# Cross-attention decoder on one core: Q and K projected densely and packed by selection matmuls, layer-norm endings on GpSimd, new step orders

## The reference

```
x1 = LN(x  + mha(x,  x,   causal, masks))           # "self",  S
x2 = LN(x1 + mha(x1, ctx, masks))                   # "cross", C
x3 = LN(x2 + fc2(relu(fc1(x2))))                    # tail of C
y  = LN(x3 + Wo(mha(x3, ctx, biased q/k/v)) + bo)   # "outer", O, and its tail
```

## Time and profile before

| what | value |
|---|---|
| median of 3 runs | 459.49 us |
| profiled execution | 457.92 us |
| its span | 456.2 us |
| PE, DVE, ACT, POOL busy | 384.5, 354.0, 249.2, 111.1 us |
| granted PE clock, mean | 0.986 |

### The profile page before, as it was taken

The page is one execution under the profiler, slowest core; times in us unless marked ns, Lnnn a source line. Parts: engine busy times, 40 slices in busy tenths (PEclk is TensorE's granted clock), DMA queues, the critical chain, the costliest instruction groups (busy, mean ns, idle before and its releaser), DMA issues.

```text
span 456.2 us, 10986 instructions
## 1 busy us (share of the span) xinstructions
PE 384.5 (84%) x3512; PEld 280.3 (61%) x3528; DVE 354.0 (78%) x1144; ACT 249.2 (55%) x557; POOL 111.1 (24%) x261
## 2 busy tenths in 40 slices
PE   0477899887898998989989899898998999889863
PEld 0454655665666666757757677676666667667632
DVE  7456888886898887887977888888787788777753
ACT  3024455544665655655665575665665765656632
POOL 8900012111221120321312132221322122322122
PEclk9989999999999999999999999999999999999987
DMA  5022323203322122222222222222122132232310
GB/s 161 0 53 57 81 62 97 60 19 64 86 59 55 39 61 53 46 62 51 45 64 51 47 53 60 46 56 62 42 58 58 40 77 49 52 65 45 67 26 17
DMA packets 22270, 25.62 MB, mean 56 GB/s; under 512 B 3781, under 2 KB 12742, under 8 KB 22214
## 3 DMA queue, kind: packets, MB, share of 16 engines
q1 hardware_dynamic: 22214, 24.93, 24.2%
HBM read 3.61 MB, written 1.05 MB: 10 GB/s over the span
## 4 chain that ended last, share of the span: by engine, by line
PE 43%; DVE 24%; issue 12%; DMA 8%; ACT 7%; SPq 4%; DVEq 0%; POOL 0%; POOLq 0%; ACTq 0%
DVE negmax L653 10%; PE k_bank L367 7%; DMA spread<-negmax_T 7%; PE score L400 6%; PE attend L425 6%; PE o_bank L442 5%; PE o_bank L452 4%; PE q_bank L367 4%; ACT o_sb L539 3%; PE score L403 2%; ACT high_q L585 2%; DVE x L739 2%; ACT high_k L577 2%; SPq L1064 2%; DVE scaled L734 2%
## 5 line engine op out<-in xcount | busy, mean ns | idle before, releaser
L531 ACT ACTIVATE probs<-attend 128x512 f32<-128x512 f32 x192 | 112.0, 599 | 46.5 <-PE attend L425 23.8
L653 DVE TENSOR_REDUCE negmax<-score 128x4 f32<-128x512 f32 x192 | 126.8, 683 | 13.1 <-PE score L403 7.2
L425 PE MATMUL attend<-spread,packed 128*128 128x512 f32 x192 | 91.1, 479 | 18.5 <-DMA spread<-negmax_T 17.3
L400 PE MATMUL score<-spread,packed 128*128 128x512 f32 x192 | 85.9, 484 | 8.0 <-DVE negmax L653 4.5
L577 ACT ACTIVATE high_k<-k_bank,flags 128x512 fp32r<-128x512 f32 x48 | 33.0, 687 | 76.5 <-PE k_bank L367 76.5
L425 PEld LDWEIGHTS attend<-spread,packed 128*128 128x128 f32 x192 | 36.5, 191 | 33.5 <-DMA spread<-negmax_T 23.2
L400 PEld LDWEIGHTS score<-spread,packed 128*128 128x128 f32 x192 | 36.1, 192 | 30.6 <-DVE negmax L653 25.5
L367 PE MATMUL k_bank<-xc_T,w_packed 128*128 128x128 f32 x384 | 52.4, 281 | 1.8 <-ACT xc_T L558 0.5
L367 PE MATMUL q_bank<-xc_T,w_packed 128*128 128x128 f32 x384 | 52.3, 281 | 0.0
L442 PE MATMUL o_bank<-probs,v_aug 128*32 128x128 f32 x1536 | 52.1, 276 | 0.0
L367 PEld LDWEIGHTS k_bank<-xc_T,w_packed 128*128 128x128 f32 x384 | 49.1, 196 | 2.1 <-ACT xc_T L558 0.8
(11 more groups left out here) (120 smaller groups left out, 629.1 us busy)
## 6 DMA issues: line engine op xcount, KB each, us to landing
spread<-packed SPq DMA_DIRECT2D x192, 96.0 KB
out_dram<-y_out SPq DMA_DIRECT2D x16, 64.0 KB, 1.8
spread<-negmax_T SPq DMA_DIRECT2D x48, 16.0 KB
rows_sb<-rows_dram SPq DMA_DIRECT2D x1, 704.0 KB
w_sb<-weights_dram SPq DMA_DIRECT2D x1, 576.0 KB, 4.2
spread<-len_mask SPq DMA_DIRECT2D x32, 8.0 KB
packed<-len_mask SPq DMA_DIRECT2D x32, 8.0 KB
x_in<-x_dram SPq DMA_DIRECT2D x1, 512.0 KB, 3.6
```

The lines of the kernel that those rows point to most:

```text
L400: last = nc.tensor.matmul(dst[:, :], packed[:, s, 0, q, :], spread[:, s, 1, :, q, :], start=True, stop=l != SELF)
L425: last = nc.tensor.matmul(dst[:, :], packed[:, s, 1, q, :], spread[:, s, 0, :, q, :], start=True, stop=l != SELF)
L531: nc.scalar.activation(probs[:, q, :], attend_bank[q % 2][:, :], ACT.Exp, scale=float(DK) ** -0.5).then_inc(exp_done.sem, 1)
L653: nc.vector.tensor_reduce(negmax[:, :].rearrange("p (j q) -> p j q", q=QUADS)[:, :, q], score_bank[q % 2][:, :].rearrange("p (j t) -> p j ...
```

## The change

Q and K come from one dense f32 matmul each (128x128, `qk_ps`). ACT rounds them to high parts and DVE takes the low parts, both on 128x256 instead of twice 128x512. Twelve fp32r matmuls of 256 columns with 0/1 weights (`select_w`, 128x128) place the parts in packed form in two banks; ACT evacuates each (128x512), adding the ones rows as bias. The bias of O goes into ACT's and DVE's instructions as a per-partition column. The endings of the layer norms (two instructions for each) move from DVE to POOL. `v_aug` has 6 slots. The tail's PSUM moves from the Q bank into a third of the transposes' bank. The first scores take the unpacked parts, 3 matmuls for 4. All `step` orders are new, and `w_packed`, `flags` and the bias pieces go.

```diff
# PE
-    project(u + 2, 1) ... project(u + 2, 0)      # 4 + 4 matmuls, 128 columns, f32
+            def project_qk(f):
+                pe.wait_ge(xc_T_ready.sem, xc_T_ready(f))
+                pe.wait_ge(packed_ready.sem, packed_ready(f - 1))
+                for kind, ws in ((0, WQ), (1, WK)):
+                    last = nc.tensor.matmul(qk_ps[:, kind, :], w_sb[:, ws[l], :],
+                                            xc_T[:, 1 if kind and l != SELF else 0, :], start=True, stop=True)
+            def select(f, half):
+                pe.wait_ge(low_ready.sem, low_ready(f))
+                if half == 0:
+                    pe.wait_ge(v_ready.sem, v_ready(f))
+                elif layer_of(f) != OUTER:
+                    pe.wait_ge(len_chain.sem, len_chain(f, 1))
+                for q in range(2):
+                    dst = pack_bank[half][:, 2 * S * q:2 * S * q + 2 * S]
+                    for term, pair in enumerate((parts[:, Q_HIGH:K_HIGH + 1, :], parts[:, Q_HIGH:K_LOW + 1:2, :],
+                                                 parts[:, Q_LOW:K_HIGH + 1:2, :])):
+                        last = nc.tensor.matmul(dst, select_w[:, term, 2 * half + q, :, :], pair,
+                                                start=term == 0, stop=term == TERMS - 1)
# ACT
-    high_k_parts, high_q_parts: 128x512 each
+            def high_parts(f):   # waits for qk_done(f), selected(f - 1), first_done(f - 1)
+                if layer_of(f) == OUTER: # Q and K apart, 128x128 each, ACT.Identity with bias
+                else:
+                    nc.scalar.copy(parts[:, Q_HIGH:K_HIGH + 1, :], qk_ps).then_inc(high_ready.sem, 1)
+            def pack(f, half):
+                act.wait_ge(selected.sem, selected(f, half + 1))
+                act.wait_ge(attended.sem, attended(f - SLOTS))
+                nc.scalar.activation(
+                    packed[:, slot_of(f), :, 2 * half:2 * half + 2, :].rearrange("p a q s -> p q a s"),
+                    pack_bank[half][:, :].rearrange("p (q a s) -> p q a s", q=2, a=2), ACT.Identity,
+                    bias=ones[:, 0:1]).then_inc(packed_ready.sem, 1)
# DVE
-    split_k, split_q: 128x512 each; finish
+            def low_parts(f):    # waits for high_ready(f); O: two scalar_tensor_tensor of 128x128 with the bias
+                    nc.vector.tensor_tensor(parts[:, Q_LOW:K_LOW + 1:K_LOW - Q_LOW, :], qk_ps,
+                                            parts[:, Q_HIGH:K_HIGH + 1, :].bitcast(F32), ALU.subtract)
# POOL, in attention_rstd (the same in tail_rstd, to x3 or y_out)
+                nc.gpsimd.tensor_scalar(normed[:, :], scaled[:, :], rstd[:, 0:1], None, ALU.mult)
+                nc.gpsimd.tensor_tensor(x1[:, m, :], normed[:, :], rows_sb[:, LN1B, :], ALU.add)
```

More of the change, by code:

```diff
@@ L351, in project @@
                 pe.wait_ge(xc_T_ready.sem, xc_T_ready(f))
[L352 to L369, removed]
+                pe.wait_ge(packed_ready.sem, packed_ready(f - 1))
+                if l != SELF:
+                    pe.wait_ge(weights_in_2, 16)
+                for kind, ws in ((0, WQ), (1, WK)):
+                    last = nc.tensor.matmul(qk_ps[:, kind, :], w_sb[:, ws[l], :],
+                                            xc_T[:, 1 if kind and l != SELF else 0, :], start=True, stop=True)
+                last.then_inc(qk_done.sem, 1)
             def project_v(f):
@@ L382, in first_scores @@
                 pe.wait_ge(first_ready.sem, first_ready(f))
-                pe.wait_ge(packed_k.sem, packed_k(f))
-                for q in range(QUADS):
-                    last = nc.tensor.matmul(first_ps, first_q[:, H * q:H * q + H],
-                                            packed[:, slot_of(f), 1, q, :],
-                                            start=q == 0, stop=q == QUADS - 1)
+                for n, (q, k) in enumerate(((Q_HIGH, K_HIGH), (Q_HIGH, K_LOW), (Q_LOW, K_HIGH))):
+                    last = nc.tensor.matmul(first_ps, first_q[:, q, :], parts[:, k, :], start=n == 0, stop=n == 2)
                 last.then_inc(first_done.sem, 1)
@@ L499, in step @@
                 transpose_o(u)
+                first_scores(u + 3)
+                select(u + 3, 0)
+                select(u + 3, 1)
                 tail(u - 1, 2)
-            pe.wait_ge(weights_in, 16)
-            pe.wait_ge(pool_setup, N_POOL_SETUP)
-            pe.wait_ge(dve_setup, N_DVE_SETUP)
-            for kind in range(4):
-                last = nc.tensor.matmul(k_bank[:, kind:kind + 1], flag_row[0:1, kind, :, :], one_sb[:, :],
-                                        start=True, stop=True)
-            last.then_inc(bias_ps, 1)
-            pe.wait_ge(bias_done, 1)
+                score(u + 2, 0)
+                attend(u + 1, 0)
+                attend(u + 1, 1)
+                score(u + 2, 1)
+                score(u + 2, 2)
+                tail(u, 0)
+                attend(u + 1, 2)
+                front_transpose(u + 4)
+            pe.wait_ge(weights_in, 16)
+            pe.wait_ge(ident_ready, 2)
+            pe.wait_ge(select_ready, 5)
             run_steps(step, -AHEAD - 3, UNITS + 5)
@@ L618, in _ @@
-            last.then_inc(weights_packed, 1)
-            act.wait_ge(bias_done, 1)
+                pack(u + 3, 0)
+                pack(u + 3, 1)
+                exponentials(u + 1, 0)
+                exponentials(u + 1, 1)
+                tail_evac(u, 0)
+                evacuate_x_T(u + 4)
+                exponentials(u + 1, 2)
+            act.wait_ge(ident_ready, 2)
+            act.wait_ge(select_zero, 1)
+            for term in range(TERMS):
+                nc.scalar.copy(select_w[:, term, :, :, DK * term:DK * term + DK],
+                               ident[:, :].rearrange("p (j q k) -> p q j k", j=BLOCKS, q=QUADS)).then_inc(select_ready, 1)
@@ L684, in split_q @@
[L684 to L697 removed]
+                dve.wait_ge(high_ready.sem, high_ready(f))
```

430 lines of the change are left out of this document (174 added, 256 removed).

## The result

The changed kernel takes 438.93 us (median of 4 runs, 438.03 to 440.2) beside 459.62 for the kernel before on the same chip: ratio 0.954, 95% interval 0.948 to 0.960. The forecast was 416 with a range of 398 to 438. The sign was right, the gain somewhat under half of what was forecast: 20.7 us in place of 43.5. The profiled execution took 439.48 us, its span 437.8.

What follows compares the result with a forecast made beforehand. No engine alone bound it: about 1.4 us of each 8.57 us step was PE waiting in a ring with DVE. 457.9 less 38.5 (steps to 7.75) and 5 (ends) gives 414.4, median 416; range 398 to 438.

Steps and rivals of the forecast that it cites:

- x2's lateness: GpSimd's 1.9 us chain to x2 delays tail(u,0) on PE by up to 0.5 us in a third of steps.
- the sum: Total time: profiled 457.9 us less 38.5 for 47 steps and 5 for the ends, 414.4; median 1.6 higher, 416.
- the others 7.6: Steps without S masks take 7.6 us, S steps 8.0, for a mean of 7.75.
- The forecast of the rings: Three dependency loops of nearly one length (PE's order, DVE, the maxima's way) give a mean step of 7.75 us, before 8.57.
- Selection, 1.38 us: Twelve 256-column passes on PE for Q and K at 0.115 us each, 1.38 us a step.
- PE's sum: PE's own work per mean step goes from 7.15 to 6.8 us, in S from 8.1 to 7.7.
- rival 1: SP's queue issues the maxima's DMA late, adding 0.5 us a step: 8.25 a step, 439 us; chance 0.15.
- ring (c): The maxima's way from their transpose through DMA, attend, exponentials, copies, values and V: 7.1 us, 0.23 more for S.
- Rival 2: Rings hide in each other and only PE is left: 7.3 us a step, 395 us; chance 0.16.
- Rival 3: Port lock shared by VectorE and GpSimd slows VectorE's two-input instructions, 0.2 us a step, 10 us: 426; chance 0.10.
- Rival 4: Slower: select's weight loads don't hide behind 256-column passes, 0.26 us each instead of 0.115: 498 us; chance 0.05.
- The ends, -5: Start and end outside the steps: earlier start less 0.8 us for two POOL endings, net -5 us, between 0 and -8.

Runs made afterwards that it cites:

- reads x1: Changed kernel, with the tail's transpose of a C unit reading x1 instead of x2 (result not the reference's): 423.86 us, ratio 0.919.
- the later tail: Changed kernel, with tail(u,0) behind project_qk(u+4) instead of ahead of attend(u+1,2), its copy and waits moved along: 416.35 us, ratio 0.905.
- own bank: Changed kernel, with the first scores in attend bank 1 instead of pack bank 1: 434.91 us, ratio 0.943.
- the two runs with a third of the selection: 4 of 12 selection matmuls kept, low parts left out: 434.3 us against the changed kernel's 438.67; 411.08 against 413.15 with the later tail and own bank.
- shorter start: Against the 413 us kernel (the later tail, own bank): v_aug cleared on GpSimd, third spread slot cleared behind GpSimd's step -3: 408.31 us, ratio 0.889.

## Why the prediction was wrong, by its steps

**The step that failed: x2's lateness, priced "up to 0.5 us late in a third of the steps".** It was seen as the one place where GpSimd's endings lie on the path, and it was mis-sized: 14.8 us over 16 C steps are 0.93 us a step (reads x1), near twice the price, and the sum has no term for it: C steps stand there among "the others 7.6" and took 8.86. In the C step shown, the forecast's own numbers read so. The chain of four GpSimd instructions was counted as 1.9 us and took 2.5 from mean and variance to x2; 0.35 of the difference are the pauses ahead of its instructions, which were not counted, 0.23 the first addition. It began 1.7 us behind `transpose_o` (forecast 2), and x2 was there 4.1 behind it. PE was done with its scores at 204.90 plus a pass of 0.23, 3.4 us behind `transpose_o`, where 3.5 to 4 was taken. With 0.15 from x2's write to the transpose that makes 0.9 us.

The forecast of the rings is right once the tail is moved: 7.75 us a step forecast, 7.75 measured in the run with the later tail (364.15 us from 40.91 to 405.06 in 47 steps). That kernel is not the one forecast, so this is evidence for the rings, not for the prediction. That its time, 416.35, is also the forecast's 416 is in part luck: its ends gave 2.8 us where 5 was forecast, and its median lies 0.35 under its profiled execution where the sum added 1.6.

Groups of the changed kernel that bear on this and on what follows (count | busy us, mean ns | idle before):

```profile
L384 PEld LDWEIGHTS pack<-parts,select_w 128*128 128x128 f32 x576 | 75.6, 195 | 5.8 <-issue 5.8
...
L840 POOL TENSOR_SCALAR var_eps<-mean_var 128x1 f32<-128x1 f32 x32 | 15.0, 469 | 73.2 <-DVE mean_var L732 73.2
...
L736 DVE SCALAR_TENSOR_TENSOR scaled<-y,mean_var,rows_sb 128x128 f32<-128x128 f32 x64 | 21.9, 342 | 0.4
...
L697 DVE TENSOR_TENSOR parts<-pack,parts 128x256 fp32r<-128x256 f32 x32 | 13.4, 418 | 6.5 <-ACT parts L591 6.4
...
L475 PE MATMUL t_bank<-ident,x 128*128 128x128 f32 x16 | 4.8, 301 | 12.3 <-POOL x L854 8.3 <-DVE mean_var L732 4.1
```

The epsilon addition on one column (L840) takes 469 ns as a mean. Before, 27 of its 32 took 0.22 to 0.23 us (the mean of 304 comes from five at the start, beside VectorE's bias pieces), as this one:

```profile
201.93 0.22 POOL L898 TENSOR_SCALAR var_eps<-mean_var 128x1 f32<-128x1 f32 x1 [6.95 <-DVE mean_var L730]
```

Both this addition and VectorE's centring, which has two SBUF inputs, wait for the same mean and variance. In the old order maxima stood ahead of the centring; in the new one it follows at once, so the two run side by side. In 31 of 32 cases the addition ended 0.08 to 0.09 us behind the centring, after 0.37 to 0.53 us; the one without a centring beside it took 0.23. The centring kept its time (L736: 342 ns, before 354).

The Trainium skill ("SBUF — State Buffer", "SBUF: two separate sides") gives the shared port pair to whichever of the two starts first and lets the other wait. Eight of the 31 agree plainly: the centring began 0.06 us ahead, and the addition was held. In the other 23 the addition's record begins 0.09 to 0.10 ahead of the centring and it is held all the same; VectorE's last `length_mask` instruction was then under way, and whether that one has the port isn't shown here. The forecast had weighed the rule for VectorE's side alone. That the port is the cause is argued from these rows; no run moved the centring by itself.

**Selection, 1.38 us.** Most starts lie 0.113 to 0.125 us apart, near the forecast 0.115; the first pair of a unit is 0.17 to 0.20 apart, and in S and C the pair behind the wait between the halves 0.19. The two halves' weight loads:

```profile
201.73 0.77 PEld L384 LDWEIGHTS pack<-parts,select_w 128*128 128x128 f32 x6
...
202.69 0.78 PEld L384 LDWEIGHTS pack<-parts,select_w 128*128 128x128 f32 x6 [0.20 <-issue]
```

Six loads take 0.77, and 0.20 us lie before the second half. That is the wait for `length_mask`: the sixth and the seventh selection start 0.30 us apart in S and C, 0.12 in O, and 0.12 everywhere in the run with an own bank. From the first start to the end of the last pitch a unit's selection takes 1.74 us in C and in most S, 1.51 in O, a mean of 1.66 in place of 1.38; the wait is worth 3.8 us by the run without it. But two thirds of all selection matmuls are worth no more than that, so PE's sum, on which the forecast spent most of its working, hardly enters the time.

**VectorE and ScalarE.** `low_parts` 0.418 us (forecast 0.45), packs 0.688 (0.60 to 0.69). Right. Of GpSimd's 0.4 us over the forecast, 0.17 a step are the stretched additions (32 of 0.25 us each).

**The way of the maxima, rival 1.** The time forecast for SP's queue, 439, is what was measured, by another mechanism: that the two agree is chance. `attend` waits for the DMA that the earlier trace rows show. The row in the list of waits of the kernel before (engine and line that waits, what for: us in all, times, longest):

```profile
PEld attend L425 <- DMA spread<-negmax_T: 23.2, 30, 3.4
```

That row and two others in the list of the changed kernel:

```profile
ACT tail_T L527 <- PE t_bank L475: 20.1, 25, 2.8
...
PEld attend L432 <- DMA spread<-negmax_T: 7.7, 16, 2.0
...
PE t_bank L475 <- POOL x L854: 8.3, 10, 1.0
```

The rival needed the second row to grow, and it shrank to a third.

The traces also settle the queue itself: in the changed kernel SP issues each DMA of the maxima 0.03 us behind the end of ScalarE's copy, as a mean of 48, and 0.23 at most. In the kernel before it was 0.41 as a mean, over 0.1 in 31 of 48, and up to 3.34, so SP's queue was late in the old order and is not in the new one.

The third row is PE's wait for x2 where the profile names it (8.3 us in ten of the 16 C steps; with the other six 12.3), the first is ACT's wait for the transpose behind it, 14.9 us of it in C steps.

A rival's time that fits is no evidence for it; its wait has to be there. The DMA of the maxima does become the limit once the tail is late no more and selection is cut, but with SP free: it is then the length of the way, ring (c), and not the queue.

**Rival 2** (PE is all that is left, 395) is out: see the two runs with a third of the selection. **Rival 3** (the lock, 10 us on VectorE) is out for VectorE: its centring takes 342 ns. **Rival 4** (slower by exposed loads) is out: 0.12 to 0.13 us a matmul, no 0.19.

**The ends, -5.** They gave -2.9. Start of the changed kernel:

```profile
11.65 2.62 DVE L826 MEMSET v_aug<- 128x3072 f32 x1 [0.59 <-issue]
...
14.71 0.27 ACT L566 COPY xc_T<-t_bank 128x128 f32<-128x128 f32 x1 [9.72 <-DVE v_aug L828]
...
16.80 0.42 DVE L697 TENSOR_TENSOR parts<-pack,parts 128x256 fp32r<-128x256 f32 x1 [2.24 <-ACT parts L591]
18.59 0.23 POOL L911 TENSOR_TENSOR first_q<-parts,head_mask 128x32 fp32r<-128x32 f32 x1
...
28.41 0.64 PE L407 MATMUL score<-spread,packed 128*128 128x512 f32 x1
```

The first transpose is evacuated at 14.71 in place of the forecast 13, since VectorE stands for 0.8, 0.8 and 0.59 us between its clears, which the forecast had put end to end. And GpSimd, which I had not followed at the start, clears the third slot of `spread` ahead of the first `first_q`: its input is there at 17.22, it starts at 18.59. First scores at 28.41, 3.1 earlier than in the earlier trace rows where 5.6 was forecast. The shorter start won 4 us, more than was missing here.

**Of the 22.9 us missed,** 22.8 lie in the steps (47 of 8.24 us for 7.75) and 2.1 in the ends; 2.1 come off because the median lies 0.5 under the profiled execution where the sum added 1.6 to it. Of the steps' 22.8, 14.8 are the x2 wait (shown by the run that reads x1) and 3.8 the wait for `length_mask` (shown, less what it would win with x2 in time). The other 4 stay open.

What brought the gain is not taken apart: the dense projections, the selection and the new orders, SP's among them, were only tried together. By themselves only the GpSimd endings were tried, and they cost time.

The best version, the later tail with the first scores' own bank and the shorter start, takes 408.3 us, 0.889 of the kernel before and 30 us less than the change as it was made.

## What to carry to other kernels

Work that leaves a busy engine for an idle one has to be priced by who waits for its result, in the order of the waiting engine, and not by the busy time it moves: GpSimd's endings made the old order 25 us slower, x2's alone held the new one up by 12 to 15, and by nothing once one transpose stood a place later. What is queued behind the new work on the idle engine counts too, as `first_q` did. Look at steps by kind before looking at the mean: a mean of 8.24 hid 7.8 and 8.9. And when several rings have nearly one length, halving one engine's work tells more than its busy share: PE was 88% busy, and two thirds of its selection were free.

## What the runs showed of the hardware

A GpSimd addition on one column (L861, 0.22 us at 200.83 in the C step above, 231 ns as a mean) took 0.51 us as L840 at 203.48, beside VectorE's `length_mask` instruction, begun 0.17 us ahead of it, and the centring, begun 0.09 behind it; it ended 0.09 us behind the centring, which kept its 0.33 us. In the earlier trace rows it was the other way round: GpSimd began 0.06 us before VectorE and kept its time, and VectorE's instruction took 0.55 us. So either engine can be the one that is held.

fp32r matmuls of 256 columns, each with its own 128-wide weight load of 195 ns, followed mostly at 0.113 to 0.125 us in the steps. Those of the first two units, behind a PE that had stood, started 0.213 us apart:

```profile
19.18 2.87 PE L384 MATMUL pack<-parts,select_w 128*128 128x256 f32 x12
```

From the third unit on (33.93 us) it was 0.12. The distance is what 256 columns would take at one column a cycle and 1.2 GHz, the lower of the clock's two levels (256 / 1.2 = 213 ns, an estimate); but the granted clock of that stretch (10 to 30 us) is given as 1.00, so by these records it was not throttled. Records and spacing disagree here, and no run settles it.
